# Row scatters and early gathers of two expert layers, in groups of four with a wait after each group

## The reference

```python
# first expert layer (block 0): two experts of eight per token, plus a shared one
scores = softmax(xt @ gate_w.T); topk_w, topk_i = top_k(scores, 2)
for e in range(8):
    y = y + comb[:, e:e+1] * ((silu(xt @ w1[e]) * (xt @ w3[e])) @ w2[e])
y = y + (silu(xt @ sw1) * (xt @ sw3)) @ sw2
# second expert layer (block 1): one expert of eight per token
top1 = argmax(softmax(x @ router_W + router_b))
h = relu(x @ W1[e] + b1[e]); y = h @ W2[e] + b2[e]; out = gates * y
```

## Time and profile before

| | us |
|---|---|
| median of three runs | 2727.16 (2722.9 to 2727.49) |
| time of the profiled execution | 2730.44 |
| its span (first to last instruction) | 2728.6 |
| PE busy | 2551.9 (94%) |
| POOL busy | 625.4 (23%) |
| mean granted TensorE clock | 0.977 of full speed |

### The profile page before, as it was taken

The page is one execution under the profiler, slowest core; times in us unless marked ns, Lnnn a source line. Parts: engine busy times, 40 slices in busy tenths (PEclk is TensorE's granted clock), DMA queues, the critical chain, the costliest instruction groups (busy, mean ns, idle before and its releaser), DMA issues. The chain is left out here.

```text
span 2728.6 us, 47274 instructions
## 1 busy us (share of the span) xinstructions
PE 2551.9 (94%) x18498; PEld 1965.2 (72%) x18498; DVE 1458.3 (53%) x2400; ACT 994.7 (36%) x2147; POOL 625.4 (23%) x649
## 2 busy tenths in 40 slices
PE   8889996999999898979999997988999999989999
PEld 4566994666666656957888886985888886467678
DVE  4474224777777733025545556325555554379982
ACT  2252223666666421323222221223222222477741
POOL 2002002101010001013333330212333332047833
PEclk9999998999999998989999999999999999999999
DMA  9442883111110102942211212553112211012210
GB/s 290 132 138 103 289 286 101 33 47 32 42 38 17 51 1 101 327 157 80 70 59 59 70 36 103 193 195 109 64 58 66 70 59 41 1 62 86 86 43 16
DMA packets 97803, 260.04 MB, mean 95 GB/s; under 512 B 19028, under 2 KB 45368, under 8 KB 90184
## 3 DMA queue, kind: packets, MB, share of 16 engines
q1 hardware_dynamic: 86520, 240.17, 26.6%
q0 software_dynamic: 3840, 10.49, 1.2%
q10 hardware_dynamic: 7248, 6.65, 0.7%
HBM read 236.13 MB, written 21.14 MB: 94 GB/s over the span
## 5 line engine op out<-in xcount | busy, mean ns | idle before, releaser
L2193 POOL TENSOR_TENSOR buf<-buf 128x512 f32<-128x512 f32 x128 | 159.9, 1273 | 504.9 <-ACT buf L2327 504.9
L2352 DVE TENSOR_REDUCE buf<-acc 128x256 f32<-128x1024 f32 x128 | 150.8, 1220 | 219.0 <-PE acc L2220 219.0
L2253 PE MATMUL acc<-buf 128*128 128x256 f32 x1024 | 257.3, 385 | 3.6 <-ACT buf L2336 3.6
L2214 PE MATMUL acc<-buf 128*128 128x256 f32 x1024 | 236.7, 384 | 3.5 <-PEq L89 2.6
L2321 ACT COPY buf<-acc 128x256 f32<-128x256 f32 x64 | 23.8, 372 | 533.5 <-PE acc L2235 533.5
L2214 PEld LDWEIGHTS acc<-buf 128*128 128x128 f32 x1024 | 189.7, 190 | 36.6 <-issue 12.1
L2253 PEld LDWEIGHTS acc<-buf 128*128 128x128 f32 x1024 | 181.1, 190 | 37.2 <-issue 15.9
L2721 ACT ACTIVATE buf<-acc,buf 128x512 f32<-128x512 f32 x256 | 172.4, 686 | 75.2 <-DVE buf L2755 75.2
L2755 DVE TENSOR_REDUCE buf<-acc 128x1 f32<-128x512 f32 x256 | 158.9, 683 | 65.1 <-PE acc L2633 65.1
L2365 DVE TENSOR_TENSOR buf<-acc,buf 128x1024 f32<-128x1024 f32 x128 | 150.8, 1219 | 67.8 <-ACT buf L2321 67.8
L2645 PEld LDWEIGHTS acc<-identity,buf 128*128 128x128 f32 x1024 | 115.0, 141 | 83.9 <-issue 78.1
(11 more groups left out here) (420 smaller groups left out, 4804.9 us busy)
## 6 DMA issues: line engine op xcount, KB each, us to landing
buf<-in_L_ffn_W SPq DMA_DIRECT2D x52, 1024.0 KB, 7.3
buf<-in_ctx SPq DMA_DIRECT2D x48, 768.0 KB, 4.3
buf<-in_ctxT SPq DMA_DIRECT2D x64, 512.0 KB, 3.9
buf<-in_L_ffn_w SPq DMA_DIRECT2D x36, 704.0 KB
buf<-state_rows SPq DMA_DIRECT2D x32, 512.0 KB
buf<-in_ctxT SPq DMA_DIRECT2D x96, 128.0 KB, 4.1
buf<-in_L_ffn_w SPq DMA_DIRECT2D x18, 640.0 KB
buf<-in_ctxT SPq DMA_DIRECT2D x32, 256.0 KB, 5.0
```

The source lines that it names most:

```text
L2193: pool.tensor_tensor(quarters[:, 2 * n:2 * n + 2, :], t[:, 4 * n:4 * n + 2, :], t[:, 4 * n + 2:4 * n + 4, :], ALU.add).then_inc(adding, 1)
L2214: pe.matmul(acc_s[:, n, :], ct0[x][:, tile(key_tile(n))], q0[:, b, 4 * y:4 * y + 4, :], start=(n % 2 == 0), stop=False)
L2253: pe.matmul(acc_m[:, 0:ROWS], ctx[x][:, key_tile(n), 0:P], probsT[y][:, n, :], start=(n == 0), stop=(n == KT - 1))
L2352: dve.tensor_reduce(most_of[n][:, :], acc_s[:, 4 * n:4 * n + 4, :].rearrange("p k r -> p r k"), AX.X, ALU.max).then_inc(part_most, 1)
```

## The change

After every fourth scatter, except the last four of a layer, POOL waits until every scatter so far of the layer has landed. In the first layer (K = 2) that is after j = 1, 3 and 5, in the second (K = 1) after j = 3. In the first layer POOL also waits, after the fourth early gather, until the first four have landed. Nothing else differs, and the third layer is as before.

```diff
@@ routed_experts, GpSimd's program @@
                     for k in range(K):
                         pool.indirect_dma_start(chip.sent_rows, bass.IndirectOffsetOnAxis(row_int[:, k, j:j + 1], axis=0),
                                                 xn[:, j, :], None).then_inc(scattered, 16)
+                    if K * (j + 1) % 4 == 0 and j < NT - 1:
+                        pool.wait_ge(scattered, sent + 16 * K * (j + 1))
 
                 if K == 2:
                     pool.wait_ge(earlier_written, 2)
@@
                                                 bass.IndirectOffsetOnAxis(row_int[:, 1, j:j + 1], axis=0)
                                                 ).then_inc(chip.gathered_early[j // 4], 16)
+                        if j == 3:
+                            pool.wait_ge(chip.gathered_early[0], 64)
                 pool.wait_ge(all_written, 1)
```

## The result

The changed kernel takes 2733.06 us (median of 10 runs, 2729.19 to 2735.41), the kernel before 2726.78 us (10 runs, 2720.64 to 2731.02). The ratio is 1.0024, 95% interval 1.0013 to 1.0034: some 6.3 us slower. The forecast was +5.8 us and 2733.0 us, with 2727 to 2740 as its range. One execution of all that follow, of 11210 us in e9_busy_pauses, was a slow one and stands in no ratio.

What follows compares the result with a forecast made beforehand. PE works 94% of the span and layers follow each other, so any uncovered delay PE waits for counts whole. Terms 3.3 + 1.0 + 1.5 = +5.8 us, on the median 2727.2 giving 2733.0 us, range 2727.0 to 2740.0.

Steps and rivals of the forecast that it cites:

- What bounds the three places: First-layer scatters have 3.7 us of cover before PE's take; second-layer scatters and first-layer early gathers have none.
- The hidden step: First layer: weights(1) come 7.0 us later behind the waits, but some 11 us remain for their load, so no cost.
- First layer's scatters: Three first-layer scatter waits add 3.6 + 3.4 = 7.0 us; past the 3.7 cover, +3.3 (between +0.6 and +5.7).
- That price of 1.7 is already paid: First layer: PE's clock already fell after the shorter pause, so nothing was added for the longer one.
- the cover of 3.7: First layer: tokens land at 260.3, PE's first take starts at 263.98 after DVE's add, leaving 3.7 us to absorb delay.
- Second layer: One scatter wait delays the fifth scatter by 4.9 us; tokens land +1.0 later (low -0.4, high +5.4 with the clock).
- a fall of the clock in this pause: Second layer, before take(1): PE's clock falling there would show the prediction failing; priced at 1.7 us.
- Gathers: First layer's early gather wait delays late gathers and DVE's adds by +1.5 us, bounds 1.42 and 2.88.
- Short waits: Rival, not slower: every wait costs an unhindered 1.42 us; total +2.0, time 2729.2 us; chance 0.27.
- Long waits: Rival, more slower: groups stay behind weights, each wait 2.88 us, second layer's clock falls; +14.0, 2741.2 us; chance 0.17.
- the likeliest case: The forecast itself, whole kernel: +4 to +8.5 us, chance 0.50, with no clock cost added.
- A gain: Rival: held-back scatters let weights land earlier; nothing over 0.2% expected; chance 0.06 with other shifts, 0.04 of it faster.

Runs made afterwards that it cites:

- e9_busy_pauses: Changed kernel with PE kept busy in its two long pauses by 14 and 12 products of zeros; ratio to the kernel before 1.0042.
- e10: Kernel before with 3 products of zeros before the first layer's first take and 6 before the second layer's take(1); ratio 0.9998.
- e11: Changed kernel run once more, unchanged; ratio to the kernel before 1.0029.
- e5: Changed kernel with SP holding first-layer weights(0) and second-layer weights(1) until four scatters landed; no ratio, first scatter to tile 1's up products 42.43 us.
- e1: Kernel before with only the first layer's three scatter waits; no ratio, first scatter to tile 1's up products 41.87 us.
- e6: Kernel before with the second layer's token loads issued ahead of weights(1); ratio to the kernel before 0.9995.
- e8: Kernel before without the third layer's three scatter waits; ratio to the kernel before 0.9998.
- e12: Kernel before with second-layer token loads ahead of weights(1), third-layer scatter waits removed, 3 products of zeros before the first take; ratio 1.0024.

## Why the prediction was right

Its steps, by the stretches:

- *What bounds the three places.* Right in each: the take's releaser changed from DVE to the token load, DVE's late adds moved with POOL, and PE's pause before take(1) grew. The hidden step, weights(1) behind the same wait, stayed hidden: the first layer's tile 1 follows tile 0 with no idle time.
- *First layer's scatters, +3.3.* The sum of the waits was forecast as 7.0 (3.6 + 3.4) and measured as 6.99 (4.20 + 2.79). Packets of q0 read off gave the first wait to within 0.6 us. The stretch shows +3.73: 3.26 up to the take, and 0.47 more from slower take and products. Two readings were true of the profile of before and not of the kernel. "That price of 1.7 is already paid": four of six executions without waits do not pay it. And the cover of 3.7: in five of the six the take starts 0.9 earlier. Against the mean of the six the term is 5.5.
- *Second layer, +1.0.* Measured +1.65 against the profile of before, +2.0 against the mean of those without a wait. The gap was 5.38 where 4.9 was taken, tokens were issued 2.66 later where 1.8 was taken, and landed sooner (2.1 us after their issue, 2.4 taken): PE's take came 1.50 later. The prediction named a fall of the clock in this pause as a sign that it fails, and priced it at 1.7. The fall came. That it did not show in the difference was luck: the profile of before had the same fall in its pause of 2.33 us (up products 5.44, 3.81 with the clock up), a row that the prediction did not use.
- *Gathers, +1.5.* Measured +2.01: the wait added 1.92, between the 1.42 and 2.88 of the bounds, and no slack took any of it.
- *The sum*, 5.8, came out as 7.4 in the stretches, 9.5 if the parts are taken against the means of undisturbed profiles (A 5.5; B 25.7 - 23.7 = 2.0; C 124.1 - 122.1 = 2.0; e10 is left out of B's mean, since its late gathers waited 1.1 us more for ACT), and 6.3 in the timed runs (interval 3.5 to 9.3; on e11's chip 4.9 to 11.2, so that 9.5 lies just outside the first and inside the second). The forecast was low in all three terms, by what weight loads add to a wait, by the clock and by the cover. So the right mechanism put it in the right place, but that the median meets it to 0.1 us is luck.
- *The rivals.* Short waits: refuted by 4.50 and 5.68. Beside fresh weight loads a wait is long, and e5 moves the long gap with them. That the DMA engines serve the queues by turns of a packet (the Trainium skill, DMA: Bandwidth & Descriptors, Queues, rings and completion order) would make it short; these waits do not agree with that. Long waits: the second and third wait of the first layer were of the short kind in all four profiles with these waits and the weights in their place (changed kernel, e1, e9, e11: 1.69 to 1.71). The clock, which stood in that rival alone, fell in the likeliest case too. A gain: all three stretches became longer.

## What to carry to other kernels

A wait for a DMA's landing, put between DMAs of one queue, costs one landing time each (here 1.4 us over the ordinary gap), and two and a half to four times that (3.7 to 5.5 us) when bulk loads have just been issued to the same DMA engines; it did not shrink from four transfers in the group to two. Before adding one, look for what covers the last transfer of the chain, count the cover against the sum of all waits, and leave a group of slack: waiting for the group before the last cost nothing here. A pause of PE is dearer than its length when the clock falls in it. One profile does not tell whether a short pause pays that, nor how large a cover is; several executions do.

## What the runs showed of the hardware

- POOL's gap at a wait among scatters was 1.69 to 1.74 us without other traffic, for groups of two as of four, except at the third layer's second wait, where it ranged from 1.74 to 3.18; beside weight loads it was 4.0 to 5.8 us.
- A pause of PE of 1.35 us was followed by a fall of the clock in e6 and by none in e8 (1.36 us), with the same program and the same work of PE ahead of it. The fall costs 1.6 us in tile 0's up products (7.22 against 5.60).
- DVE's adds stood for 3.3 to 4.5 us while POOL issued the last of 16 indirect DMAs without a pause, in three of eight profiles (before, e10, e12), and PE's take then came 0.9 us later. The cause is open.
- Executions of kernels that are alike up to there differ by up to 8 us in when the first expert layer begins (229.9 to 238.0 us), more than the whole change costs.
